# Macaron block on eight cores: the LayerNorm's bf16 cast from GpSimd to VectorE, and a seventh weight slot

## The chip, the cores and the metric

The kernel runs on the eight cores of one Trainium2 chip. Each core works on four of the 32 sequences and exchanges nothing with the others. The metric is the device time of the slowest core in microseconds (us). In this text PE is TensorE, DVE is VectorE, ACT is ScalarE, POOL is GpSimd and SP is SyncE, which issues most of the DMAs.

## The reference

`x` has 32 sequences of 2048 tokens with 1024 channels. The block is half an FFN, attention with latent heads, and half an FFN again, each on the LayerNorm of `x` and added to `x`:

```python
x = x + 0.5 * ffn(layernorm(x), weight, disha)
x = x + attn(layernorm(x), ...)
x = x + 0.5 * ffn(layernorm(x), weight, disha)

def layernorm(x, eps=1e-5):
    m = mean(x); v = var(x)
    return (x - m) / sqrt(v + eps)

def ffn(x, weight, disha):            # r = 64
    result = einsum('bsd,od->bso', x, weight)
    pooled = x.reshape(..., D // r, r).sum(axis=-2)
    return result + pooled @ disha
```

`attn` makes q, k and v with 16 heads of 64, maps each to 32 latent dimensions, rotates q and k, takes a causal softmax and projects back.

## The kernel before

**Layout.** Channels lie on the 128 partitions, in eight chunks of 128, tokens in the columns. A core works on one half sequence at a time (`hb`, 1024 tokens), eight times in all. The half's `x` stays in `x_sb` as float32. Every stage outside attention works on tiles of 512 tokens, `tt` = 0 and 1.

**Stages of one half sequence.** LayerNorm of tile 0, first FFN of tile 0, LayerNorm, attention projection (`emit_cattn`) of tile 0, then the same for tile 1; attention over 16 heads in pairs; the output projection (`emit_cproj`) in two segments of 512 columns; the second FFN in two passes, tile 0 and tile 1, with `store=True`. In the second FFN the result goes through the two halves of `stg` to HBM, and POOL issues the DMA that brings the next half sequence's `x` into the place that has become free (L649).

**A group.** An FFN stage has eight output chunks `o`. Each is a group of eight matmuls into one of two PSUM banks, over the eight input chunks in `ln_sb`. DVE then empties the bank and adds `x` (L657 in the first FFN, L632 in the second, L1011 in the output projection). The attention projection has sixteen such groups, `m` = 0 to 15: 0 to 3 are q, 4 to 7 k, 8 to 15 v. What follows on a group there (rope, norms, transposes of v) is put off by two groups. The v bias row is L789, the copies of the transposed v are L812.

**LayerNorm.** `ln_stats_chunk` does one chunk: a cast of `x` to bf16 into `xb_sb` (L555), its square into one of two halves of `sq_sb` (L558), and two matmuls with a column of ones that sum both over the channels (L563 and L568). `ln_finish` makes mean and scale from the sums (L575 to L600) and writes `ln_sb` in two DVE rows per chunk (L603, L607). The statistics of the next LayerNorm are woven into the stage before it: behind group `o` stands chunk `o - 3`, and the chunks 5, 6 and 7 follow the last group:

```python
            if ln_next is not None and o >= 3:
                ln_stats_chunk(ln_next, o - 3, sqb=lnbank)
        if ln_next is not None:
            ln_stats_chunk(ln_next, 5, sqb=lnbank)
            ln_stats_chunk(ln_next, 6, sqb=lnbank)
            ln_stats_chunk(ln_next, 7, sqb=lnbank)
```

In the attention projection of tile 0 the chunk `m - 8` stands ahead of group `m`, for `m` from 8 on. Six stages of a half sequence carry such chunks: both tiles of the first FFN, the projection of tile 0, the second segment of the output projection, and both passes of the second FFN (in the last half sequence only the first of them, as nothing follows).

**Order and waits.** There is no scheduler. Each engine runs its instructions in the order in which the program writes them. The class `Prog` keeps, for every tile, the last writer and its readers, and puts waits on semaphores ahead of an instruction that needs them. An engine has one semaphore that counts its finished instructions.

**Weights.** `stream_slot` loads the weights of one group (256 KB) over SP's queue into the next of `NSLOT` slots of `wslot`; a load waits until the group that used the slot before is done. Each slot has a semaphore of its own (`SL0`, ...).

Of the kernel before, what the change touches and what calls it, by code (L numbers as in the profile page):

```python
# [38 lines left out]
class Prog:  # L39
# [6 lines left out]
                 "ST0", "ST1", "ST2", "ST3", "ST4", "ST5", "ST6", "ST7",  # L46
                 "PF0", "PF1", "PF2", "PF3", "PF4", "PF5", "PF6", "PF7",
                 "PE", "DV", "AC", "PL",
                 "SL0", "SL1", "SL2", "SL3", "SL4", "SL5")

    def __init__(self):
        self.streams = {e: [] for e in self.ENGINES}
# [146 lines left out]
def build_program(bpc, seq):  # L199
# [49 lines left out]
    def sb(name, shape, dt):  # L249
        return st.enter_context(nc.sbuf_tensor(name, shape, dt))  # L250
# [35 lines left out]
    r_sb = sb("r_sb", [1, 2 * QW], F32)  # L286
    r_bf = sb("r_bf", [1, 2 * QW], BF16)
    rb_sb = sb("rb_sb", [64, 2 * QW], BF16)
    NSLOT = 6
    wslot = sb("wslot", [128, NSLOT * 1024], BF16)  # L290
    stg = sb("stg", [128, 1024], F32)
    build_sb = sb("build_sb", [128, 1024], BF16)
# [47 lines left out]
    p = Prog()  # L340
    BK = [p.R("bank", i) for i in range(8)]

    def bank_ap(i, lo, hi):
        return PS[:, 512 * i + lo:512 * i + hi]
# [3 lines left out]
    def stream_slot(src_ap, src_res):  # L348
        j = slot_ctr[0] % NSLOT
        slot_ctr[0] += 1  # L350
        r = p.R("slot", j)
        p.op("sync", lambda eng, s=src_ap, j=j: eng.dma_start(
            out=wslot[:, 1024 * j:1024 * j + 1024], in_=s),
            reads=[src_res], writes=[r], dma="SL%d" % j)
        return j, r
# [191 lines left out]
    def x_ap(o, hb_local_cols):  # L547
        lo, hi = hb_local_cols
        return x_sb[:, HALF * o + lo:HALF * o + hi]

    def ln_stats_chunk(tt, c, sqb=6):
        g0 = TTA * tt
        par = c % 2
        xres = p.R("x", c, tt)
        p.op("gpsimd", lambda eng, c=c, g0=g0: eng.tensor_copy(  # L555
            xb_sb[:, TTA * c:TTA * c + TTA], x_ap(c, (g0, g0 + TTA))),
            reads=[xres], writes=[p.R("xb", c)])
        p.op("gpsimd", lambda eng, c=c, par=par: eng.tensor_tensor(  # L558
            sq_sb[:, TTA * par:TTA * par + TTA],
            xb_sb[:, TTA * c:TTA * c + TTA],  # L560
            xb_sb[:, TTA * c:TTA * c + TTA], ALU.mult),
            reads=[p.R("xb", c)], writes=[p.R("sq", par)])
        p.group("tensor", [lambda eng, c=c: eng.matmul(  # L563
            bank_ap(0, 0, TTA)[0:1, :], ones128_sb[:],
            xb_sb[:, TTA * c:TTA * c + TTA],
            start=(c == 0), stop=(c == NCH - 1))],
            reads=[p.R("xb", c), p.R("ones128")], writes=[BK[0]])
        p.group("tensor", [lambda eng, c=c, par=par, sqb=sqb: eng.matmul(  # L568
            bank_ap(sqb, 0, TTA)[0:1, :], ones128_sb[:],
            sq_sb[:, TTA * par:TTA * par + TTA],  # L570
            start=(c == 0), stop=(c == NCH - 1))],
            reads=[p.R("sq", par), p.R("ones128")], writes=[BK[sqb]])
# [41 lines left out]
    def emit_ffn(b, hb, tt, ln_next=None, lnbank=6, store=False, nxt=None):  # L614
        g0 = TTA * tt
        for o in range(NCH):
# [11 lines left out]
            if store:  # L628
# [15 lines left out]
                if nxt is not None:  # L644
                    if tt == NT - 1 and o >= 3:
                        ln_stats_chunk(0, o - 3, sqb=3)
                    nb2, nhb2 = nxt
                    p.op("gpsimd", lambda eng, b2=nb2, hb2=nhb2, o=o, g0=g0:
                         eng.dma_start(  # L649
                             out=x_sb[:, HALF * o + g0:HALF * o + g0 + TTA],  # L650
                             in_=d_x[b2, 128 * o:128 * o + 128,
                                     HALF * hb2 + g0:HALF * hb2 + g0 + TTA]),
                         writes=[p.R("x", o, tt)],
                         dma="PF")
# [6 lines left out]
# [6 lines that stand above are left out]
# [499 lines left out]
def run(inputs, bpc, seq, n_cores):  # L1166
    x = np.asarray(inputs["L0_attn_x"], dtype=np.float32)
    B = x.shape[0]
    assert B == bpc * n_cores
    sh = _prep_shared(inputs, seq)  # L1170
    nc = build_program(bpc, seq)
    in_maps = []
    for c in range(n_cores):
        m = dict(sh)
        m["x"] = np.ascontiguousarray(
            x[bpc * c:bpc * (c + 1)].transpose(0, 2, 1))
        in_maps.append(m)
    res = run_bass_kernel_spmd(nc, in_maps, core_ids=list(range(n_cores)))
    outs = [np.asarray(r["out"]) for r in res.results]
    out = np.concatenate(outs, axis=0)  # L1180
    return np.ascontiguousarray(out.transpose(0, 2, 1))
# [4 lines left out]
```

How the kernel before makes its waits and increments, by code:

```python
        def body(eng):  # L180
            for e in stream:
                if e[0] == "w":
                    eng.wait_ge(sems[e[1]], e[2])
                else:
                    ins = e[1](eng)
                    if e[2] is not None:
                        ins.then_inc(sems[e[2]], e[3])
# [923 lines left out]
        def body(eng):  # L1111
            for e in stream:
                if e[0] == "w":
                    eng.wait_ge(sems[e[1]], e[2])
                else:
                    ins = e[1](eng)
                    if e[2] is not None:
                        ins.then_inc(sems[e[2]], e[3])
```

## Time and profile before

| what | us |
|---|---|
| timed runs | 5708.12 and 5788.53 |
| their median | 5748.33 |
| the profiled execution's own time | 5726.87 |
| its span on the slowest core (core 1) | 5725.3 |
| spans of the eight cores | 5683.0 to 5725.3 |

The span reaches from the first to the last instruction on one core, and the execution's own time is that of the slowest core with what lies around it, 1.6 us here. All views are of core 1. Its span holds about 410 us of start (weights are folded and written back to HBM in the order in which they are streamed later), and eight half sequences. "Idle before" in a row is the time for which the engine stood still just ahead of it, with what ended the wait.

### The profile page before, as it was taken

The page shows a single profiled execution, that of the slowest core. Times are in us where ns is not written, and L with a number is a line of the kernel's source. Part 1 is how long each engine was busy: PE and PEld are TensorE (multiplying, and loading weights), DVE is VectorE, ACT ScalarE, POOL GpSimd, SP SyncE. Part 2 cuts the span into 40 slices and gives each one's busy share as a digit, 9 for nine tenths or more (in the row PEclk, how much of TensorE's full clock was granted, in tenths as well). Part 3 has the DMA queues.
Part 4 walks back from the last instruction along what each step waited for, and adds up shares of the span by engine and source line. Part 5 has one row for each costly group of instructions (what it writes and reads, how often), then busy time and mean ns, then how long its engine had stood idle before and what let it go on. Part 6 is the DMA issues. An engine that isn't in the chain of part 4 may idle for free.

```text
span 5725.3 us, 58087 instructions; the slowest of 8 cores (5683.0 to 5725.3 us)
## 1 busy us (share of the span) xinstructions
PE 3783.0 (66%) x13322; PEld 1183.6 (21%) x13322; DVE 1944.4 (34%) x4078; ACT 1671.6 (29%) x1938; POOL 694.0 (12%) x884
## 2 busy tenths in 40 slices
PE   0116666677776666667776666667776666676877
PEld 0002212222221212122221222122221221122222
DVE  1115432531124433451123533352123543253113
ACT  0000350026620052007630043005650035003662
POOL 0012002200022101310013100310003200320001
PEclk9996657776676756786776756677667765776667
DMA  3241003210022102210012101310003100311002
GB/s 86 66 141 50 30 1 104 62 45 1 1 74 81 56 1 63 89 53 7 1 49 94 57 12 30 107 57 17 1 15 111 57 28 3 119 58 31 1 1 78
DMA packets 152516, 277.09 MB, mean 48 GB/s; under 512 B 34322, under 2 KB 34322, under 8 KB 152210
## 3 DMA queue, kind: packets, MB, share of 16 engines
q1 hardware_dynamic: 124818, 210.44, 12.6%
q0 software_dynamic: 8960, 29.37, 1.7%
q10 hardware_dynamic: 18432, 33.56, 1.6%
q8 instruction: 148, 2.42, 0.2%
q14 instruction: 158, 1.29, 0.1%
HBM read 231.36 MB, written 46.14 MB: 48 GB/s over the span
## 4 chain that ended last, share of the span: by engine, by line
PE 48%; DVE 16%; issue 15%; ACT 10%; DMA 6%; POOL 3%; SPq 1%; DVEq 1%; ACTq 0%; POOLq 0%
PE PS L907 12%; PE PS L868 11%; PE PS L621 8%; PE PS L693 7%; ACT PT L880 4%; PE PS L1001 4%; DVE ln_sb L603 3%; DMA stg<-w_attn 3%; DVE rb_sb L953 3%; ACT r_sb L928 2%; POOL sq_sb L558 2%; DVE y_sb L958 1%; PE PS L568 1%; PE PS L563 1%; PE PS L802 1%
## 5 line engine op out<-in xcount | busy, mean ns | idle before, releaser
L880 ACT ACTIVATE PT<-PS,b_exp 128x1024 bf16<-128x1024 f32 (+7 forms) x1536 | 1254.6, 863 | 718.3 <-PE PS L868 691.3
L907 PE MATMUL PS<-PT,v_store 128*65 128x512 bf16 (+3 forms) x2560 | 927.9, 480 | 228.1 <-DVE y_sb L958 207.9
L868 PE MATMUL PS<-q_store,k_store 32*128 32x512 bf16 (+3 forms) x2560 | 772.0, 475 | 325.9 <-ACT PT L880 308.3
L621 PE MATMUL PS<-ln_sb,wslot 128*128 128x512 bf16 x2048 | 676.1, 475 | 176.8 <-DVE ln_sb L607 139.4
L886 DVE TENSOR_TENSOR PT<-PT,causal_sb 128x128 bf16<-128x128 bf16 x1024 | 230.9, 226 | 1504.3 <-ACT PT L880 1495.2
L693 PE MATMUL PS<-ln_sb,wslot 128*128 128x512 bf16 x2048 | 645.1, 463 | 91.8 <-DVE ln_sb L607 91.8
L555 POOL CAST xb_sb<-x_sb 128x512 bf16<-128x512 f32 x384 | 244.8, 637 | 3568.0 <-DVE x_sb L1011 2746.4
L575 ACT ACTIVATE m_bf<-PS 1x512 bf16<-1x512 f32 x48 | 28.2, 587 | 1876.3 <-PE PS L563 1843.6
L558 POOL TENSOR_TENSOR sq_sb<-xb_sb 128x512 bf16<-128x512 bf16 x384 | 399.3, 1040 | 951.1 <-PE PS L568 910.1
L907 PEld LDWEIGHTS PS<-PT,v_store 128*65 128x65 bf16 x2560 | 292.2, 136 | 777.3 <-issue 709.6
L868 PEld LDWEIGHTS PS<-q_store,k_store 32*128 32x128 bf16 x2560 | 180.7, 98 | 927.3 <-issue 905.2
L621 PEld LDWEIGHTS PS<-ln_sb,wslot 128*128 128x128 bf16 x2048 | 219.5, 112 | 611.8 <-issue 517.4
L693 PEld LDWEIGHTS PS<-ln_sb,wslot 128*128 128x128 bf16 x2048 | 209.9, 111 | 466.7 <-issue 353.5
L1001 PE MATMUL PS<-y_sb,wslot 128*128 128x512 bf16 x1024 | 246.9, 399 | 42.6 <-DVE y_sb L958 31.7
L953 DVE CAST rb_sb<-PS 64x1024 bf16<-64x1024 f32 x128 | 157.0, 1227 | 298.8 <-PE PS L947 295.9
L563 PE MATMUL PS<-xb_sb,ones_sb 128*1 128x512 bf16 x384 | 161.8, 421 | 138.5 <-POOL xb_sb L555 133.1
L568 PE MATMUL PS<-sq_sb,ones_sb 128*1 128x512 bf16 x384 | 167.4, 436 | 117.6 <-POOL sq_sb L558 116.7
L632 DVE SCALAR_TENSOR_TENSOR stg<-PS,x_sb 128x512 f32<-128x512 f32 x128 | 88.6, 692 | 419.4 <-PE PS L621 361.5
L749 ACT ACTIVATE sqq_sb<-PS 128x512 bf16<-128x512 f32 x64 | 38.2, 597 | 540.5 <-DVE q_store L744 540.5
L607 DVE TENSOR_TENSOR ln_sb<-ln_sb,ab_sb 128x512 bf16<-128x512 bf16 x384 | 176.0, 458 | 41.0 <-DVE ln_sb L603 1.4
L603 DVE TENSOR_TENSOR ln_sb<-xb_sb,mb_sb 128x512 bf16<-128x512 bf16 x384 | 172.0, 448 | 0.2
L657 DVE SCALAR_TENSOR_TENSOR x_sb<-PS,x_sb 128x512 f32<-128x512 f32 x128 | 88.5, 692 | 236.2 <-PE PS L621 234.2
(103 smaller groups left out, 2241.3 us busy)
## 6 DMA issues: line engine op xcount, KB each, us to landing
wslot<-me_strm SPq DMA_DIRECT2D x256, 256.0 KB, 2.7
wslot<-wa_strm SPq DMA_DIRECT2D x256, 256.0 KB, 2.5
wslot<-cp_strm SPq DMA_DIRECT2D x128, 256.0 KB, 2.6
out<-stg ACTq DMA_DIRECT2D x128, 256.0 KB, 3.1
x_sb<-x POOLq DMA_DIRECT2D x112, 256.0 KB, 4.2
stg<-w_attn SPq DMA_DIRECT2D x48, 256.0 KB
x_sb<-x SPq DMA_DIRECT2D x8, 512.0 KB
wa_strm<-build_sb SPq DMA_DIRECT2D x16, 256.0 KB
```

The costliest lines, as they stand in the source:

```text
L555: p.op("gpsimd", lambda eng, c=c, g0=g0: eng.tensor_copy(xb_sb[:, TTA * c:TTA * c + TTA], x_ap(c, (g0, g0 + TTA))), reads=[xres], writes=[ ...
L558: p.op("gpsimd", lambda eng, c=c, par=par: eng.tensor_tensor(sq_sb[:, TTA * par:TTA * par + TTA], xb_sb[:, TTA * c:TTA * c + TTA], xb_sb[: ...
L568: p.group("tensor", [lambda eng, c=c, par=par, sqb=sqb: eng.matmul(bank_ap(sqb, 0, TTA)[0:1, :], ones128_sb[:], sq_sb[:, TTA * par:TTA * p ...
L603: p.op("vector", lambda eng, c=c: eng.tensor_tensor(ln_sb[:, TTA * c:TTA * c + TTA], xb_sb[:, TTA * c:TTA * c + TTA], mb_sb[:], ALU.subtract),
L621: fns.append(lambda eng, j=j, dd=dd, bk=bk: eng.matmul(bank_ap(bk, 0, TTA), slot_ap(j, dd), ln_sb[:, TTA * dd:TTA * dd + TTA], start=(dd = ...
L693: fns.append(lambda eng, j=j, dd=dd, bk=bk: eng.matmul(bank_ap(bk, 0, TTA), slot_ap(j, dd), ln_sb[:, TTA * dd:TTA * dd + TTA], start=(dd = ...
L868: hg=hg, gq=gq: eng.matmul(PS[:, 1024 * par + a:1024 * par + bnd], k_store[32 * hg:32 * hg + 32, seq * gq + 128 * c:seq * gq + 128 * c + 128],
L880: eng.activation(PT[:, QW * slot + qoff:QW * slot + QW], PS[:, 1024 * par + qoff:1024 * par + QW], AF.Exp, bias=b_exp[:, 0:1]),
L886: p.op("vector", lambda eng, slot=slot, qoff=qoff: eng.tensor_tensor(PT[:, QW * slot + qoff:QW * slot + qoff + 128], PT[:, QW * slot + qof ...
L907: yb=yb: eng.matmul(PS[0:65, yb + a:yb + bnd], v_store[:, 1040 * c + 65 * h:1040 * c + 65 * h + 65], PT[:, QW * slot + a:QW * slot + bnd], ...
L953: p.op("vector", lambda eng, yb=yb, par=par: eng.tensor_copy(rb_sb[:, QW * par:QW * par + QW], PS[64:128, yb:yb + QW]), reads=ybanks, writ ...
L1001: eng.matmul(bank_ap(bk, 0, hi - lo), slot_ap(j, dd), y_sb[:, QW * dd + lo:QW * dd + hi], start=(dd == 0), stop=(dd == NCH - 1)))
```

## The change

The cast of `ln_stats_chunk` is issued on DVE in place of POOL. The square stays on POOL. `NSLOT` goes from 6 to 7, with a semaphore `SL6` and 2 KB more of SBUF in each partition.

```diff
-                 "SL0", "SL1", "SL2", "SL3", "SL4", "SL5")
+                 "SL0", "SL1", "SL2", "SL3", "SL4", "SL5", "SL6")
...
-    NSLOT = 6
+    NSLOT = 7
...
-        p.op("gpsimd", lambda eng, c=c, g0=g0: eng.tensor_copy(
+        p.op("vector", lambda eng, c=c, g0=g0: eng.tensor_copy(
             xb_sb[:, TTA * c:TTA * c + TTA], x_ap(c, (g0, g0 + TTA))),
             reads=[xres], writes=[p.R("xb", c)])
```

DVE's queue in the first FFN stage (tile 0 of the first half sequence), before; the words in brackets are the semaphores that a row waits for (PE, DV, AC and PL are those of the engines, PF that of a prefetch of `x`):

```order
L657 SCALAR_TENSOR_TENSOR x_sb<-PS,x_sb 128x512 [waits PE] x8
L578 TENSOR_TENSOR msq<-m_bf 1x512 [waits AC]
L581 SCALAR_TENSOR_TENSOR var_f<-PS,msq 1x512 [waits PE,DV]
L598 CAST mb_sb<-PS 128x512 [waits PE]
```

The same place now:

```order
L657 SCALAR_TENSOR_TENSOR x_sb<-PS,x_sb 128x512 [waits PE] x4
L555 CAST xb_sb<-x_sb 128x512 [waits DV,PL]
L657 SCALAR_TENSOR_TENSOR x_sb<-PS,x_sb 128x512 [waits PE]
L555 CAST xb_sb<-x_sb 128x512 [waits DV,PL]
L657 SCALAR_TENSOR_TENSOR x_sb<-PS,x_sb 128x512 [waits PE]
L555 CAST xb_sb<-x_sb 128x512 [waits DV,PL]
L657 SCALAR_TENSOR_TENSOR x_sb<-PS,x_sb 128x512 [waits PE]
L555 CAST xb_sb<-x_sb 128x512 [waits DV,PL]
L657 SCALAR_TENSOR_TENSOR x_sb<-PS,x_sb 128x512 [waits PE]
L555 CAST xb_sb<-x_sb 128x512 [waits DV,PL] x4
L578 TENSOR_TENSOR msq<-m_bf 1x512 [waits AC]
```

A cast stands behind the emptying of each bank from the fourth on, and four stand behind the last one. PE's queue keeps its order.

PE's queue there, in the changed kernel, around the group behind the first statistics:

```order
L621 MATMUL PS<-ln_sb,wslot 128x512 x7
L563 MATMUL PS<-xb_sb,ones_sb 1x512 [waits DV]
L568 MATMUL PS<-sq_sb,ones_sb 1x512 [waits PL]
L621 MATMUL PS<-ln_sb,wslot 128x512 [waits SL0,PE]
L621 MATMUL PS<-ln_sb,wslot 128x512 x7
```

The first statistics matmul waits for DVE's semaphore, where it waited for POOL's, and the next group stands behind both.

POOL's queue in the first pass of the second FFN, before, from the first four prefetches on:

```order
L649 DMA x_sb<-x 128x512 [waits DV] x4
L555 CAST xb_sb<-x_sb 128x512
L558 TENSOR_TENSOR sq_sb<-xb_sb 128x512 [waits PL,PE]
L649 DMA x_sb<-x 128x512 [waits DV]
L555 CAST xb_sb<-x_sb 128x512
L558 TENSOR_TENSOR sq_sb<-xb_sb 128x512 [waits PL,PE]
```

The same place now:

```order
L649 DMA x_sb<-x 128x512 [waits DV] x4
L558 TENSOR_TENSOR sq_sb<-xb_sb 128x512 [waits DV,PL,PE]
L649 DMA x_sb<-x 128x512 [waits DV]
L558 TENSOR_TENSOR sq_sb<-xb_sb 128x512 [waits DV,PL,PE]
L649 DMA x_sb<-x 128x512 [waits DV]
```

The casts have left the queue, and each square waits for DVE besides.

## Rows read from the trace of the kernel before

**Rows 1.** The page, first part: busy us, share of the span, instructions.
```profile
PE 3783.0 (66%) x13322; PEld 1183.6 (21%) x13322; DVE 1944.4 (34%) x4078; ACT 1671.6 (29%) x1938; POOL 694.0 (12%) x884
```
**Rows 2.** Who waited for whom: us in total, times, longest us.
```profile
POOL sq_sb L558 <- PE PS L568: 910.1, 201, 271.7
...
PE PS L568 <- POOL sq_sb L558: 116.7, 158, 1.5
...
PE PS L621 <- DMA wslot<-me_strm: 36.9, 1, 36.9
```
**Rows 3.** Timeline, first FFN of tile 0: start, duration, row, idle before.
```profile
423.76 2.28 PE L621 MATMUL PS<-ln_sb,wslot 128*128 128x512 bf16 x8
...
424.32 1.04 POOL L558 TENSOR_TENSOR sq_sb<-xb_sb 128x512 bf16<-128x512 bf16 x1 [1.67 <-DVE x_sb L657]
...
426.14 0.69 DVE L657 SCALAR_TENSOR_TENSOR x_sb<-PS,x_sb 128x512 f32<-128x512 f32 x1 [2.13 <-PE PS L621]
426.21 0.44 PE L568 MATMUL PS<-sq_sb,ones_sb 128*1 128x512 bf16 x1
...
426.58 2.27 PE L621 MATMUL PS<-ln_sb,wslot 128*128 128x512 bf16 x8
```
**Rows 4.** Timeline, end of the same stage.
```profile
434.60 0.69 DVE L657 SCALAR_TENSOR_TENSOR x_sb<-PS,x_sb 128x512 f32<-128x512 f32 x1 [2.13 <-PE PS L621]
...
437.06 1.04 POOL L558 TENSOR_TENSOR sq_sb<-xb_sb 128x512 bf16<-128x512 bf16 x1 [0.21 <-PE PS L568]
...
438.35 0.42 PE L568 MATMUL PS<-sq_sb,ones_sb 128*1 128x512 bf16 x1 [0.82 <-POOL sq_sb L558]
```
**Rows 5.** Groups by line: busy us, mean ns of one, idle before.
```profile
L555 POOL CAST xb_sb<-x_sb 128x512 bf16<-128x512 f32 x384 | 244.8, 637 | 3568.0 <-DVE x_sb L1011 2746.4 <-DVE x_sb L657 457.9 <-DVE c_eff L992 304.1
...
L607 DVE TENSOR_TENSOR ln_sb<-ln_sb,ab_sb 128x512 bf16<-128x512 bf16 x384 | 176.0, 458 | 41.0 <-DVE ln_sb L603 1.4
...
L527 DVE CAST build_sb<-stg 128x1024 bf16<-128x1024 f32 x8 | 5.6, 694 | 36.1 <-DMA stg<-cprojT 36.1
```
**Rows 6.** Windows, DVE rows that write `ln_sb`: length, DVE busy, PEclk, DMA.
```profile
377.00:385.00 8.00, 6.18 (x16) 1.00 0.54 122
443.00:453.10 10.10, 8.48 (x16) 0.50 0.00 1
```
**Rows 7.** Window, line L693 alone, q groups: PE busy, PEld busy, PEclk, DMA.
```profile
462.00:487.50 25.50, 14.80 (x40) 4.48 (x40) 0.65 0.14 42
```
**Rows 8.** Timeline, second FFN, first pass.
```profile
937.93 0.58 POOL L649 DMA_DIRECT2D x_sb<-x  x1 [5.27 <-DVE stg L632]
938.51 0.62 POOL L555 CAST xb_sb<-x_sb 128x512 bf16<-128x512 f32 x1
939.34 1.03 POOL L558 TENSOR_TENSOR sq_sb<-xb_sb 128x512 bf16<-128x512 bf16 x1 [0.21 <-POOL xb_sb L555]
...
941.14 3.59 PE L621 MATMUL PS<-ln_sb,wslot 128*128 128x512 bf16 x8
```
**Rows 9.** Timeline, attention projection of tile 0, around `m` = 8.
```profile
489.46 2.28 PE L693 MATMUL PS<-ln_sb,wslot 128*128 128x512 bf16 x8
...
491.83 0.65 DVE L764 TENSOR_TENSOR k_store<-t_sb 128x512 bf16<-128x512 bf16 x1
```
**Rows 10.** The same stage, a v group.
```profile
512.64 0.74 DVE L789 TENSOR_SCALAR v_sb<-PS,b_vo 128x512 bf16<-128x512 f32 x1
512.80 2.27 PE L693 MATMUL PS<-ln_sb,wslot 128*128 128x512 bf16 x8
```
**Rows 11.** Windows: length, busy of PE, PEld, DVE, ACT, POOL, PEclk, DMA.
```profile
1138.00:1166.00 28.00, 23.46 (x80) 7.27 (x80) 12.18 (x24) 0.59 (x1) 12.85 (x16) 0.80 0.28 76
1057.00:1133.00 76.00, 51.50 (x232) 17.82 (x232) 47.58 (x97) 2.98 (x5) 13.25 (x16) 0.81 0.20 56
...
1663.00:1720.00 57.00, 34.35 (x80) 9.03 (x80) 10.95 (x23) 0.59 (x1) 17.54 (x24) 0.58 0.35 111
1726.00:1765.00 39.00, 27.35 (x81) 7.98 (x81) 11.49 (x24) 0.59 (x1) 17.60 (x24) 0.72 0.55 176
```

The windows are, in this order: first FFN of tile 1, attention projection of tile 0 and, of the second half sequence, first and second pass of the second FFN.

## The prediction

> **What bounds the kernel now.** I began with the page's first part: POOL is busy for 12% of the span [rows 1], so an engine-by-engine share would call its load harmless, and moving the 384 casts a matter of taste. The view of who waited for whom says where to look instead: POOL's square waits 910.1 us in 201 places for TensorE's own statistics matmul, and TensorE waits only 116.7 us in 158 places for the square [rows 2]. So POOL runs ahead of TensorE and stands waiting for a free square buffer (there are two). The timeline of one FFN stage shows this in detail [rows 3]: the square of a later chunk starts at 424.32, while TensorE is still in the group of 423.76. When the group is done, the two statistics matmuls (the second at 426.21) find their inputs ready, and the next group of eight follows at 426.58, which is 0.44 us after VectorE began to empty the bank of the group before (426.14). TensorE is the bound inside these stages, and the statistics cost it only their own matmuls. What lets POOL run ahead is that its queue holds only statistics (and, in the second FFN, prefetches): a cast there starts as soon as its x chunk exists, whatever VectorE has still to do.
>
> **What the change does to that order.** A chunk's statistics (number o-3) stand behind group o in the program. On VectorE the cast now stands behind the emptying of group o's bank, which waits for TensorE to end group o. POOL's square waits for the cast, TensorE's second statistics matmul waits for the square, and group o+1 stands behind that matmul. A chain that was loose by three groups becomes a closed ring: group, emptying, cast, square, statistics, next group.
>
> **An ordinary FFN stage, step by step.** From the start of the emptying: 0.69 for it [rows 3], 0.43 for the cast, 0.2 to hand over to POOL (the gap of 0.21 ahead of the square of 437.06 [rows 4]), 1.04 for the square [rows 3], 0.25 from its end to the matmul (437.06 + 1.04 to 438.35 [rows 4]), and 0.37 from that matmul to the next group (426.21 to 426.58 [rows 3]). That is 2.98 us, where 0.44 stands now: 2.5 us more per group.
> The cast's price on VectorE is not in the trace for this tile. The same conversion between the same memories for 1024 columns takes 694 ns [rows 5]; halved it is 0.35, undivided 0.69. I take 0.43, between the half and the 458 ns that VectorE's multiply of a 128x512 tile takes [rows 5], and keep both ends.
> Four of the five stalled groups (o = 3 to 6) delay a group: 4 x 2.5 = 10.0 us. Behind o = 7 come the casts and squares of chunks 4 to 7. Today the last square starts 2.46 us after the last emptying began and its matmul 3.75 us after it [rows 4], because POOL had only two chunks left. Now all four squares come behind the first cast: 0.69 + 0.43 + 0.2 + 4 x 1.04 + 0.25 = 5.7, or 2.0 more.
>
> **Shared memory port.** The sixteen normalising rows of a LayerNorm took 6.18 us with POOL idle, and 8.48 us with POOL casting beside them [rows 6]. In the tail VectorE's casts of chunks 5 to 7 now meet POOL's squares. If they only queue politely it costs nothing; if a cast waits for a square each time, three casts add up to 3 x 0.4 = 1.2 us. I take 0.8 for each tail. The same rows give something back: ahead of the attention projection of tile 0 those casts are gone, and with them 8.48 - 6.18 = 2.3 us.
> The Trainium skill, SBUF — State Buffer, section "SBUF: two separate sides", says that VectorE and GpSimd share a port pair as an exclusive lock that is held for the whole instruction. The 2.3 us [rows 6] agree. By that rule alone each tail would pay the full 1.2 us instead of 0.8, some 16 us more over the kernel.
>
> **TensorE's clock.** A ring of 5.3 us with 2.3 us of group in it looks like today's q part of the attention projection, where five groups (40 matmuls) stand in 25.5 us. They took 14.80 us of it at a granted clock of 0.65 [rows 7], 2.96 us per group, against 2.28 in the FFN stage [rows 3]. So the chip went back and forth between its two levels, 1.2 and 2.4 GHz, and I charge 0.7 us for each delayed group. The ends are 0 (it stays at the upper level) and 1.3 (the lower one throughout: 3.59 us per group [rows 8]).
>
> **Sums for one half sequence (there are 8).**
> First FFN, both token tiles, and the output projection's second segment, three stages of one kind: 4 x (2.5 + 0.7) + 2.0 + 0.8 = 15.6 us each, 46.8.
> Attention projection of tile 0: eight chunks, from m = 8 on. For m = 8 the cast stands behind the rope work of m = 7, whose last row starts at 491.83; the next VectorE row could start about 0.55 later, so the group comes at 492.4 + 0.43 + 0.2 + 1.04 + 0.25 + 0.37 = 494.7, where it is 489.46 now [rows 9]: 5.2. For the other seven, from the start of the v bias row: 0.74 + 0.43 + 0.2 + 1.04 + 0.25 + 0.37 = 3.0 where 0.16 stands now [rows 10]: 2.8 each, 19.6. With 8 x 0.7 for the clock and 2.3 back: 28.1.
> Second FFN, first pass: here the ring exists already, since POOL must first issue the prefetch of x, which waits for the emptying: issue 0.58, cast with its hand-over 0.83, square, all in a row on POOL [rows 8]. The cast leaves that row: -0.83 for each of five chunks, and -0.8 for each of the last three, -6.5; with 0.8 for the port, -5.7.
> Second FFN, second pass: 39 us now at a clock of 0.72 [rows 11]. It becomes a stage like the first FFN's after the change: 28 + 15.6 = 43.6 [rows 11], and the emptying, which now holds TensorE up, waits at times for a store; +6, from 0 to +10.
> Together 75.2, times 8 is 602. In the last half sequence nothing is prefetched: its first pass gains no 5.7 but loses 15.6, and the second pass has no statistics: 602 + 21.3 - 6 = 617 us.
>
> **What costs nothing.** The seventh weight slot: TensorE waited for a weight load once, 36.9 us before the first FFN, for the first load [rows 2]; one more load in flight shortens no wait. At the start of the program the casts come behind VectorE's weight folding, some 12 us later than now (an estimate: eight squares of 1.04 us in a row, with their hand-overs), and that same 36.9 us wait covers them; without it they would cost those 12 us. Attention holds no cast at all.
>
> **Total.** The profiled execution ran 5726.9 us (span 5725.3); the two timed runs gave 5708.1 and 5788.5, median 5748.3, so the sum stands on a run from their lower part. 5726.9 + 617 = 6344; I say 6340.
> Bounds: 24 stalled groups and chunks per half sequence, 192 in all. The cast at 0.35 or 0.69: -15 or +50. The clock, 160 groups, 0 or 1.3: -112 or +96. The port, 40 tails, 0 or 1.2: -32 or +16. The second pass: -42 or +28. All low 6143, all high 6534.
>
> **Rivals.**
> Full clock: TensorE keeps the upper level through the rings. For it: the attention projection as a whole ran at 0.81 [rows 11]. Against it: [rows 7]. 6340 - 112 - 20 (second passes) = 6208, say 6210. Chance 0.20.
> Low clock: the ring holds TensorE at 1.2 GHz as the first pass of the second FFN is held now (clock 0.58 [rows 11], groups of 3.59 us). 6340 + 96 = 6436. Chance 0.18.
> Faster, by the second FFN: that first pass takes 57 us where the first FFN's stage takes 28 for the same matmuls [rows 11]. If POOL, rid of the casts, no longer held it up, 29 x 7 = 203 us would go. This wins from the point where a ring costs less than 203 / 192 = 1.06 us per group instead of 2.5, that is, if the casts could slip in ahead of the emptying. With 0.4 us per group (the cast alone) the time is 5727 - 203 + 77 = 5600. Against it: the prefetch issue stays on POOL, behind the emptying [rows 8], and the cast cannot pass a row ahead of it. Chance 0.03.
> The Trainium skill, GPSIMD Engine Reference, section "Key points", calls VectorE structurally about twice as fast for elementwise work. The trace agrees on the single cast (637 ns on POOL, 694 for twice the columns on VectorE [rows 5]), and that is the argument for this rival.
> No change: the squares' chain is hidden after all and gains and losses cancel, 5727. For it: POOL's large idle share [rows 1]. Chance 0.03.
> A ring as worked out here, with a mixed clock, has 0.56; its own range is 6260 to 6420.
>
> **Numbers.** Slower by over 2% (about what can be told from no change) holds the forecast and both clock rivals, 0.94; within 2% 0.03; faster 0.03. The range 6160 to 6490 takes in both clocks and most of the bounds; attention may also shift by itself, for which I have no price.
>
> **What would show it.** In the changed profile the wait of the statistics matmul L568 for the square should be the largest of TensorE's (some 192 waits of about 1 us), with one for the cast beside it. The emptying should be followed by the cast, the square and the group at 0.7, 1.3 and 3.0 us. The FFN stage should take 43 us instead of 28, the projection of tile 0 104 instead of 76, the first pass 51 instead of 57, attention the same. The forecast is wrong if TensorE starts a group while the square before it still runs, or if the first pass falls to 30 us.

## The result, and the profile after

The changed kernel takes 6494.9 us (median of 11 runs, 6473.6 to 6520.5), the kernel before 5730.1 us (10 runs, 5708.1 to 5788.5). The ratio is 1.132, with an interval from 1.128 to 1.136: 765 us slower. In some executions of any of these kernels the cores of one die show a lower granted clock and the time is about 1% longer; the times and ratios of all runs below are medians of the other executions. Direction and mechanism came as forecast. The size did not: 6495 lies 155 us above the predicted 6340 and 5 us above the upper end of the range.

The page's first part, as in [rows 1] (engine, busy us, share of the span, instructions; some matmul records are missing):

```profile
span 6492.0 us, 57942 instructions; the slowest of 8 cores (6447.4 to 6492.0 us)
...
PE 4070.5 (63%) x13176; PEld 1247.6 (19%) x13322; DVE 2092.4 (32%) x4462; ACT 1670.6 (26%) x1938; POOL 472.2 (7%) x500
```

VectorE got 148 us of work more, POOL 222 less, and no engine is near full. Yet TensorE, which had no instruction added, is busy for at least 287 us more. Its matmuls became longer.

Who waited for whom, as in [rows 2] (us in total, times, longest us):

```profile
POOL sq_sb L558 <- DVE xb_sb L555: 5523.8, 224, 481.4
...
PE PS L563 <- DVE xb_sb L555: 516.1, 260, 89.5
...
PE PS L568 <- POOL sq_sb L558: 263.9, 283, 1.6
```

Before, the square waited for TensorE, which had not yet read the square ahead of it. Now it waits for the cast, and TensorE waits for both. Before TensorE's first statistics matmul the emptying and the cast go by, before its second one the square. One of the 260 waits for the cast, the longest, is not of a ring: it stands at the start of the program, where VectorE folds weights first.

The timeline of the first FFN of tile 0, one ring and the end of the stage (start, duration, row, idle before):

```profile
440.06 0.69 DVE L657 SCALAR_TENSOR_TENSOR x_sb<-PS,x_sb 128x512 f32<-128x512 f32 x1 [4.93 <-PE PS L621]
...
440.67 0.42 DVE L555 CAST xb_sb<-x_sb 128x512 bf16<-128x512 f32 x1
...
441.36 1.04 POOL L558 TENSOR_TENSOR sq_sb<-xb_sb 128x512 bf16<-128x512 bf16 x1 [4.92 <-DVE xb_sb L555]
...
442.65 0.59 PE L568 MATMUL PS<-sq_sb,ones_sb 128*1 128x512 bf16 x1 [0.72 <-POOL sq_sb L558]
...
443.17 3.60 PE L621 MATMUL PS<-ln_sb,wslot 128*128 128x512 bf16 x8
...
446.87 0.69 DVE L657 SCALAR_TENSOR_TENSOR x_sb<-PS,x_sb 128x512 f32<-128x512 f32 x1 [5.78 <-PE PS L621]
...
447.48 2.27 DVE L555 CAST xb_sb<-x_sb 128x512 bf16<-128x512 f32 x4
...
448.16 4.50 POOL L558 TENSOR_TENSOR sq_sb<-xb_sb 128x512 bf16<-128x512 bf16 x4 [5.76 <-DVE xb_sb L555]
...
452.91 0.59 PE L568 MATMUL PS<-sq_sb,ones_sb 128*1 128x512 bf16 x1
```

From the start of the emptying to the cast it is 0.6 us, to the square 1.3, to the next group 3.11: the ring, where [rows 3] have 0.44 us. The group in it takes 3.60 us instead of 2.28. The period, from emptying to emptying, is 6.8 us.

Windows, as in [rows 11] (length; busy of PE, PEld, DVE, ACT, POOL; PEclk; DMA share; GB/s): first FFN of tile 1, attention projection of tile 0, second FFN's first and second pass.

```profile
1274.00:1322.30 48.30, 33.05 (x79) 8.92 (x80) 15.23 (x31) 0.79 (x2) 8.65 (x8) 0.57 0.15 44
1158.00:1269.10 111.10, 66.82 (x228) 21.05 (x231) 46.89 (x102) 3.11 (x6) 8.31 (x8) 0.67 0.13 38
1822.40:1872.60 50.20, 31.64 (x79) 9.15 (x81) 15.67 (x31) 0.59 (x1) 12.93 (x16) 0.70 0.40 126
1878.70:1928.50 49.80, 34.16 (x80) 9.04 (x81) 14.56 (x32) 0.59 (x1) 12.77 (x16) 0.57 0.47 138
```

The first FFN's stage went from a clock of 0.80 to 0.57, the projection from 0.81 to 0.67, the second pass from 0.72 to 0.57. The first pass, which had a ring before, went from 0.58 to 0.70. These are single stages, and the first FFN's 0.57 is the lowest of its eight in tile 1. The mean over the first seven half sequences went from 0.78 and 0.79 (first FFN, tile 0 and tile 1) to 0.70 and 0.67, from 0.79 to 0.67 in the projection of tile 0, from 0.75 to 0.59 in the second pass, and from 0.61 to 0.67 in the first.

With every stage's length read from TensorE's rows, mean over half sequences 2 to 8 (the last half sequence, in which nothing is prefetched, is in them; without it the first pass went from 57.4 to 51.3 us and the second from 38.2 to 50.1):

| stage, us | before | after | early cast (E3) | statistics first (E4) | both (E5) |
|---|---|---|---|---|---|
| first FFN, tile 0 | 29.2 | 46.8 | 27.5 | 28.4 | 28.7 |
| projection, tile 0 | 77.2 | 112.5 | 75.8 | 76.6 | 75.6 |
| first FFN, tile 1 | 28.1 | 46.5 | 27.3 | 28.1 | 28.6 |
| projection, tile 1 | 74.5 | 73.9 | 74.1 | 73.9 | 74.4 |
| output projection | 36.7 | 55.7 | 36.1 | 36.6 | 38.1 |
| second FFN, first pass | 53.6 | 50.9 | 47.6 | 36.0 | 33.3 |
| second FFN, second pass | 36.2 | 46.5 | 32.5 | 37.2 | 33.4 |

The differences between the first two columns add up to 97.3 us, times 8 is 778. The first half sequence lost less, 77 us, so that all eight give 759. The normalisations between the stages took 21 us more, and attention, 2356 us in all before and 2341 after, takes 15 off: with 1 us at the start that is the 767 us between the two profiled spans. The stages that carry casts are nearly all of it; the projection of tile 1, which carries none, stayed. Attention's 15 us are no gain that can be told: among the cores of the kernel before it differs by 26 us.

### The profile page after: what moved, and what is told of

Read it like the earlier page. It is cut to its first block, busy times and chain, and to the rows that moved or that the text cites. A ratio compares the mean times of both kernels' runs of the same rounds, so it can differ in the third digit from the quotient of the medians.

```text
span 6492.0 us, 57942 instructions; the slowest of 8 cores (6447.4 to 6492.0 us)
## 1 busy us (share of the span) xinstructions
PE 4070.5 (63%) x13176; PEld 1247.6 (19%) x13322; DVE 2092.4 (32%) x4462; ACT 1670.6 (26%) x1938; POOL 472.2 (7%) x500
## 4 chain that ended last, share of the span: by engine, by line
PE 47%; DVE 18%; issue 15%; ACT 9%; DMA 5%; POOL 4%; SPq 1%; DVEq 1%; ACTq 0%; POOLq 0%
PE PS L907 10%; PE PS L621 9%; PE PS L868 9%; PE PS L693 7%; PE PS L1001 4%; POOL sq_sb L558 4%; ACT PT L880 4%; PE PS L568 3%; DMA stg<-w_attn 3%; DVE ln_sb L607 2%; DVE rb_sb L953 2%; DVE ln_sb L603 2%; ACT r_sb L928 2%; DVE xb_sb L555 2%; DVE y_sb L958 1%
## 5 line engine op out<-in xcount | busy, mean ns | idle before, releaser
L907 PE MATMUL PS<-PT,v_store 128*65 128x512 bf16 (+3 forms) x2560 | 910.9, 472 | 227.6 <-DVE y_sb L958 208.1
L621 PE MATMUL PS<-ln_sb,wslot 128*128 128x512 bf16 x1993 | 773.3, 543 | 184.2 <-DVE ln_sb L607 148.7
L558 POOL TENSOR_TENSOR sq_sb<-xb_sb 128x512 bf16<-128x512 bf16 x384 | 410.4, 1078 | 5532.4 <-DVE xb_sb L555 5523.8
L693 PE MATMUL PS<-ln_sb,wslot 128*128 128x512 bf16 x1984 | 708.3, 509 | 83.2 <-DVE ln_sb L607 71.0
L575 ACT ACTIVATE m_bf<-PS 1x512 bf16<-1x512 f32 x48 | 28.1, 586 | 2748.4 <-PE PS L563 2748.4
L563 PE MATMUL PS<-xb_sb,ones_sb 128*1 128x512 bf16 x384 | 191.6, 499 | 516.1 <-DVE xb_sb L555 516.1
L568 PE MATMUL PS<-sq_sb,ones_sb 128*1 128x512 bf16 x384 | 204.6, 533 | 268.7 <-POOL sq_sb L558 263.9
L621 PEld LDWEIGHTS PS<-ln_sb,wslot 128*128 128x128 bf16 x2048 | 243.4, 124 | 658.6 <-issue 591.5
L693 PEld LDWEIGHTS PS<-ln_sb,wslot 128*128 128x128 bf16 x2048 | 226.9, 119 | 495.0 <-issue 410.6
L1001 PE MATMUL PS<-y_sb,wslot 128*128 128x512 bf16 x997 | 287.9, 452 | 46.5 <-DVE y_sb L958 34.3
L812 DVE COPY v_store<-PS 128x256 bf16<-128x256 bf16 x256 | 75.2, 294 | 424.6 <-PE PS L802 424.2
L555 DVE CAST xb_sb<-x_sb 128x512 bf16<-128x512 f32 x384 | 197.4, 542 | 0.9 <-issue 0.8
L1011 DVE SCALAR_TENSOR_TENSOR x_sb<-PS,c_eff,x_sb 128x512 f32<-128x512 f32 x128 | 96.1, 751 | 295.2 <-PE PS L1001 270.5
```

The source lines that it names most:

```text
L555: p.op("vector", lambda eng, c=c, g0=g0: eng.tensor_copy(xb_sb[:, TTA * c:TTA * c + TTA], x_ap(c, (g0, g0 + TTA))), reads=[xres], writes=[ ...
L558: p.op("gpsimd", lambda eng, c=c, par=par: eng.tensor_tensor(sq_sb[:, TTA * par:TTA * par + TTA], xb_sb[:, TTA * c:TTA * c + TTA], xb_sb[: ...
L621: fns.append(lambda eng, j=j, dd=dd, bk=bk: eng.matmul(bank_ap(bk, 0, TTA), slot_ap(j, dd), ln_sb[:, TTA * dd:TTA * dd + TTA], start=(dd = ...
L693: fns.append(lambda eng, j=j, dd=dd, bk=bk: eng.matmul(bank_ap(bk, 0, TTA), slot_ap(j, dd), ln_sb[:, TTA * dd:TTA * dd + TTA], start=(dd = ...
L907: yb=yb: eng.matmul(PS[0:65, yb + a:yb + bnd], v_store[:, 1040 * c + 65 * h:1040 * c + 65 * h + 65], PT[:, QW * slot + a:QW * slot + bnd], ...
L1001: eng.matmul(bank_ap(bk, 0, hi - lo), slot_ap(j, dd), y_sb[:, QW * dd + lo:QW * dd + hi], start=(dd == 0), stop=(dd == NCH - 1)))
```

## The experiments

The theory: the cast's place in VectorE's queue, behind an emptying that waits for TensorE, closes a ring, and the ring also costs clock. The rivals: the seventh slot has a part in it; VectorE has too much work or shares its port with POOL; the ring's clock costs as little as I had charged, and the rest is somewhere else.

**E1, the cast alone, and E2, the slot alone.**

```diff
# E1, from the changed kernel
-    NSLOT = 7
+    NSLOT = 6
# E2, from the changed kernel
-        p.op("vector", lambda eng, c=c, g0=g0: eng.tensor_copy(
+        p.op("gpsimd", lambda eng, c=c, g0=g0: eng.tensor_copy(
```

> The cast on VectorE with six weight slots as before. Ring theory (each group's statistics wait for emptying, cast and square in a row): all of the loss is the cast's, so 6495 us within 20, and FFN stages of 46 us as in the changed kernel. Rival (the seventh slot changes when weights land and costs or gives something): more than 30 us away from 6495.

> The seventh weight slot with the cast on POOL as before. Ring theory: 5730 us within 20, since no group waited for a weight load after the first. Rival (the slot has a price of its own): more than 30 us away from 5730.

E1 took 6493.3 us, ratio to the kernel before 1.133 (1.128 to 1.137); E2 5731.2 us, 1.0015 (0.998 to 1.005). The cast is the whole loss, and the slot is worth nothing that can be told.

**E3, the cast early.** The changed kernel, with the cast of chunk o right behind the emptying of group o, three groups ahead of its statistics. Casts, squares and matmuls are as many as in the changed kernel, and the casts stay on VectorE; squares and statistics matmuls keep their place. The second FFN and the output projection are done in the same way; `ln_cast` is the cast of `ln_stats_chunk`, split off.

```diff
+    def ln_cast(tt, c):
...
                     reads=[BK[bk], xr], writes=[xr])
+                if ln_next is not None:
+                    ln_cast(ln_next, o)
...
+            if ln_next is not None and 6 <= m < 14:
+                ln_cast(ln_next, m - 6)
             flush(m)
```

> All casts stay on VectorE, but cast c stands right behind the emptying of group c (in the attention projection ahead of the vector work of group c+6), so it is done three groups before TensorE asks for it; the squares and the statistics matmuls stay where they are. Ring theory: the place in the queue is what costs. First FFN stages go back from 46 to 28 us, the projection of tile 0 from 112 to 74, the first pass of the second FFN stays near 51 because the prefetch is still ahead of the square: 5660 us, from 5620 to 5740. Rival (384 more rows on VectorE, or their meeting with POOL at the shared port, are what costs): above 6200.

Measured: 5610.0 us, ratio 0.978 (0.974 to 0.983), 885 us less than the changed kernel with the same work on the same engines. The timeline of a first FFN's stage (E3's line numbers: L663 emptying, L554 cast, L560 square, L570 statistics, L623 group):

```profile
1862.30 0.69 DVE L663 SCALAR_TENSOR_TENSOR x_sb<-PS,x_sb 128x512 f32<-128x512 f32 x1 [0.43 <-PE PS L623]
1862.34 0.38 PE L570 MATMUL PS<-sq_sb,ones_sb 128*1 128x512 bf16 x1
...
1862.65 1.90 PE L623 MATMUL PS<-ln_sb,wslot 128*128 128x512 bf16 x8
1862.87 1.04 POOL L560 TENSOR_TENSOR sq_sb<-xb_sb 128x512 bf16<-128x512 bf16 x1 [2.16 <-PE PS L570]
1863.17 1.02 DVE L554 CAST xb_sb<-x_sb 128x512 bf16<-128x512 f32 x1 [0.17 <-DVE x_sb L663]
```

The next group starts 0.35 us after the emptying began (0.44 before the change [rows 3]), and the group takes 1.90 us: TensorE is at its upper level here. The square now runs beside the group. The cast beside it takes 1.02 us instead of 0.43 and ends 0.28 us after the square: that fits the shared port, for which I had charged 0.8 us in each tail, and here it costs nothing, since nobody waits for this cast.
The Trainium skill, SBUF — State Buffer, section "SBUF: two separate sides", has VectorE and GpSimd exclude each other for a whole instruction, if VectorE's is in a mode that uses two ports or has two inputs in SBUF. A cast that waited for all the rest of the square would have taken 0.74 + 0.43 = 1.17 us, so the trace agrees nearly, at 1.02.

So neither VectorE's load nor its meeting with POOL made the loss. VectorE is busy for longer here (2148 us) than in the changed kernel. The place in the queue made it.
The kernel is even faster than before the change, though the interval leaves open whether by more than 2%. By the table it wins 14.6 us per half sequence, 9.7 of them in the second FFN's passes, where the cast has left POOL's row of prefetch, cast and square; times 8 is 117, and 112 to 120 were measured, by which median of the kernel before is taken (5722.5 us beside this run, 5730.1 in the result above).

**E4, the statistics first.** This one is made from the kernel before, with the cast on POOL, and asks about the ring that was there already, in the second FFN's first pass: the prefetch that POOL must issue behind the emptying, ahead of the cast and the square.

```diff
                 if nxt is not None:
+                    if ln_next is not None and o >= 3:
+                        ln_stats_chunk(ln_next, o - 3, sqb=lnbank)
                     if tt == NT - 1 and o >= 3:
...
-            if ln_next is not None and o >= 3:
+            if ln_next is not None and o >= 3 and nxt is None:
                 ln_stats_chunk(ln_next, o - 3, sqb=lnbank)
```

> The kernel before, with one thing exchanged in the first pass of the second FFN: the statistics of chunk o-3 stand ahead of the prefetch of x for chunk o, as they already do in the second pass. Theory (the prefetch on POOL, which waits for the emptying, closes a ring there): the first pass falls from 57 us to between 30 and 38, 133 to 189 us less in all, 5541 to 5597. Rival (the pass is set by its traffic of stores, prefetches and weights): 57 us as before, 5730.

Measured: 5577.2 us, ratio 0.973 (0.968 to 0.978), 145 to 153 us less than the same two medians of before. The same two passes by windows (first and second pass):

```profile
1633.10:1670.30 37.20, 26.86 (x81) 7.79 (x81) 11.16 (x23) 0.59 (x1) 17.65 (x24) 0.78 0.55 170
1676.00:1715.50 39.50, 27.67 (x81) 7.90 (x81) 11.37 (x24) 0.59 (x1) 17.60 (x24) 0.76 0.55 173
```

The first pass fell from 57 us to 37, its clock rose from 0.58 to 0.78, and POOL did the same work in it (17.6 us [rows 11]).

**E5, both.** E3 and E4 in one kernel.

> Both cures at once: the casts on VectorE right behind the emptying of their group (seven slots), and in the first pass of the second FFN the statistics ahead of the prefetch. Ring theory: the two rings are independent, so the first pass falls from 47.6 us (early casts alone) to the 32.5 us of the second pass, 7 x 15 = 105 us under the 5624 of the early casts alone: 5520 us, from 5480 to 5560. Rival (the traffic of that pass is what is left): no better than the 5582 us of the statistics-first kernel.

Measured: 5491.3 us, ratio 0.959 (0.957 to 0.961), 29 us better than expected. 0.978 times 0.973 is 0.952, below the interval: most of both gains add, but each alone had already taken something out of the first pass (53.6 us to 47.6 in E3, to 36.0 in E4), and that counts once. First and second pass now take 33 us each.

**E6, TensorE kept busy.** The changed kernel, with five matmuls of 512 columns behind each group that a ring follows. Nobody reads their results.

```diff
+            if o >= 3 and (ln_next is not None or nxt is not None):
+                filler(j, 5, 7, lambda i: ln_sb[:, TTA * i:TTA * i + TTA])
...
+            if ln_next is not None and 7 <= m < 15:
+                filler(j, 5, 7, lambda i: ln_sb[:, TTA * i:TTA * i + TTA])
...
+                if si == len(segs) - 1 and o >= 3:
+                    filler(j, 5, 1, lambda i: y_sb[:, QW * i + lo:QW * i + hi])
```

> The changed kernel with five more matmuls of 512 columns behind each group that has a ring, into a PSUM bank nobody reads, while TensorE would wait for the emptying and the cast. Theory (half of the loss beyond the bare waits is TensorE at 1.2 GHz, because it stands still in each ring): the groups in the rings fall from 3.3 us to 1.9 to 2.4, about 218 of them, so the kernel gets faster by doing more: 6255 us, from 6200 to 6330, with granted clocks above 0.8 in the FFN stages. Rival (the clock is low for another reason, or the extra matmuls stand in the way): 6495 us or more.

Measured: 6206.7 us, ratio 1.084 (1.081 to 1.087), 288 us less than the changed kernel, with some 1300 matmuls more. A ring of a first FFN's stage (L665 emptying, L561 cast, L564 square, L574 statistics, L627 group, L552 the added matmuls):

```profile
574.40 1.24 PE L552 MATMUL PS<-ln_sb,wslot 128*128 128x512 bf16 x5
...
574.67 0.69 DVE L665 SCALAR_TENSOR_TENSOR x_sb<-PS,x_sb 128x512 f32<-128x512 f32 x1 [3.77 <-PE PS L627]
...
575.28 0.41 DVE L561 CAST xb_sb<-x_sb 128x512 bf16<-128x512 f32 x1
...
575.96 1.04 POOL L564 TENSOR_TENSOR sq_sb<-xb_sb 128x512 bf16<-128x512 bf16 x1 [3.75 <-DVE xb_sb L561]
...
577.25 0.38 PE L574 MATMUL PS<-sq_sb,ones_sb 128*1 128x512 bf16 x1 [0.93 <-POOL sq_sb L564]
577.56 1.90 PE L627 MATMUL PS<-ln_sb,wslot 128*128 128x512 bf16 x8
```

And a first FFN's stage of tile 1 by window, beside the changed kernel's first window above:

```profile
2022.00:2063.50 41.50, 31.29 (x105) 10.33 (x105) 14.60 (x32) 0.59 (x1) 8.63 (x8) 0.83 0.17 51
```

The ring is the same (emptying to next group 2.89 us; 2.95 in the mean over the changed kernel's first FFNs), but the group takes 1.90 us instead of 3.60, and the granted clock is 0.83 instead of 0.57 (0.84 instead of 0.67 in the mean). The FFN's matmuls by groups of lines (busy us, mean ns of one, idle before), in the changed kernel and in E6:

```profile
L621 PE MATMUL PS<-ln_sb,wslot 128*128 128x512 bf16 x1993 | 773.3, 543 | 184.2 <-DVE ln_sb L607 148.7 <-DMA wslot<-me_strm 28.7 <-issue 5.1
```

```profile
L627 PE MATMUL PS<-ln_sb,wslot 128*128 128x512 bf16 x2048 | 649.9, 460 | 161.1 <-DVE ln_sb L613 135.7 <-DMA wslot<-me_strm 25.4
```

One takes 460 ns instead of 543; in the kernel before it was 475. So what E6 takes off, 288 us, is clock, and 6207 - 5730 = 477 us is left. Of the 288 some 22 lie in first passes, whose ring was there before (the stretch of their groups went from 44.0 us to 40.8, seven times). The clock's part of the loss is thus 266 us, and the rest, 499, is waiting.

**E7, the cast twice.** The changed kernel, with each cast done twice in the same place.

> The changed kernel with each cast on VectorE done twice in a row. Ring theory: every ring gets longer by the whole second cast with its wait for the first, about 0.5 us, in 218 rings: +113 us, 6610, from 6580 to 6650. Rival (casts lie beside TensorE's work): 6495 us within 20, though VectorE is busy for another 165 us.

Measured: 6613.9 us, ratio 1.155 (1.153 to 1.158), 119 us more than the changed kernel. The timeline, the wait that took it up (L558 is the second cast, L566 the first statistics matmul), and a ring of a first pass (L635 emptying, L652 prefetch, L561 square):

```profile
438.22 0.42 DVE L555 CAST xb_sb<-x_sb 128x512 bf16<-128x512 f32 x1
...
438.74 0.43 DVE L558 CAST xb_sb<-x_sb 128x512 bf16<-128x512 f32 x1
```

```profile
PE PS L566 <- DVE xb_sb L558: 670.7, 258, 91.1
```

```profile
1888.26 0.69 DVE L635 SCALAR_TENSOR_TENSOR stg<-PS,x_sb 128x512 f32<-128x512 f32 x1 [5.35 <-PE PS L624]
...
1889.39 0.43 DVE L558 CAST xb_sb<-x_sb 128x512 bf16<-128x512 f32 x1
1889.57 0.58 POOL L652 DMA_DIRECT2D x_sb<-x  x1 [5.30 <-DVE xb_sb L555]
...
1890.17 1.05 POOL L561 TENSOR_TENSOR sq_sb<-xb_sb 128x512 bf16<-128x512 bf16 x1
```

0.52 us from cast to cast times some 220 rings (28 in each half sequence but for the last one's second pass: four in each of five stages, eight in the projection) is 114 us, and the wait for the cast grew by 155. That 114 meets 119 so closely is partly luck, since the rings do not pay alike. From emptying to next group those of the first FFN went from 2.95 us to 3.60, 0.65 in place of 0.52, and a part of that is the clock again: the second statistics matmul ran at the lower level (0.59 us, not 0.38) in 59 of 64 of these rings, in the changed kernel in 23. Those of the first pass stayed at 3.62: there POOL issues the prefetch while the second cast runs, and the square could not start before it. So what is put on VectorE between emptying and square is paid in every ring in which nothing beside it covers it.

**E8, the same remedy in the projection.** E5 with five such unread matmuls in each q step of the attention projection (64 places), where [rows 7] showed a clock of 0.65 in the kernel before.

```diff
                                 reads=[p.R("qp", qpar), p.R("wqk4bf")],
                                 writes=[BK[nb]])
+                        filler(5)
```

> On top of the early casts with the statistics first (5491 us): five matmuls nobody reads in each q step of the attention projection, between the latent product and the norm for which TensorE waits on ScalarE; 64 places. Theory (those waits keep TensorE at 1.2 GHz for about half of the q and k groups, 2.96 us per group against 2.28 or less): 0.7 to 1.0 us less per place, 45 to 64 us, so 5440 us, from 5400 to 5470. Rival (the extra matmuls stand in the way of the norm, or the clock there is held down by something else): 5490 us or more.

Measured: 5460.0 us, ratio 0.9535 (0.950 to 0.957), the best version, though its interval just touches E5's. By the groups of lines (busy us, mean ns of one, idle before), the projection's matmuls in E5 and in E8:

```profile
L703 PE MATMUL PS<-ln_sb,wslot 128*128 128x512 bf16 x2048 | 643.8, 462 | 70.4 <-DVE ln_sb L609 70.4
```

```profile
L712 PE MATMUL PS<-ln_sb,wslot 128*128 128x512 bf16 x2048 | 576.1, 423 | 70.4 <-DVE ln_sb L618 70.4
```

68 us less busy, but only some 30 us less time. The waits show one place where it went: TensorE's wait for the norm of q fell, that for the norm of k rose. First E5's two rows, then E8's:

```profile
PE PS L764 <- ACT sqq_sb L761: 143.9, 64, 3.1
...
PE PS L788 <- DVE sqk_sb L782: 62.7, 47, 2.3
```

```profile
PE PS L775 <- ACT sqq_sb L772: 96.1, 64, 2.0
...
PE PS L799 <- DVE sqk_sb L793: 84.2, 48, 2.3
```

The second grew by 21.5 us: a faster TensorE waits longer for VectorE in the k part. The 320 added matmuls are busy for 80.2 us, more than the 47.8 us by which the wait for the norm of q fell. With the matmuls of the two FFNs, 14 us shorter too (634.4 to 620.1), that makes 68 + 14 + 48 less and 80 + 21.5 more: 28 us, an estimate from one core of each run, and close to what was measured.

## Why the prediction was right, and where it was off

**The ring: right.** Predicted were 2.98 us from emptying to next group, measured 3.11 at the lower clock and 2.89 at the upper one (E6), and 2.95 in the mean of the first FFN's rings. The cast was taken at 0.43 and took 0.42. The tail was put at 5.7 + 0.8 from its emptying to the last statistics matmul, and is 6.04, so that the port's 0.8 was at most 0.3. The 2.3 us that were to come back did: the sixteen normalising rows ahead of the projection of tile 0 took 5.95 us in place of 8.48. The first pass went from 57 us to 51 as worked out. E7 shows that the ring is closed (one cast more lengthens it), E3 that only the place in the queue closes it.

**The clock: the term that was mis-sized.** "I charge 0.7 us for each delayed group" is the step that failed. I took it from the q groups of [rows 7], 2.96 us each, because a ring of 5.3 us with 2.3 us of group in it looked like them. In the changed kernel the groups in the rings took 3.1 to 3.5 us in the mean of each kind of stage, at a mean granted clock of 0.59 to 0.70 in those stages of the FFN and the projection. The length that I compared with was wrong as well: 2.28 us [rows 3] is a group of the first half sequence, and over the whole kernel before, the same groups took 1.9 to 2.1 us in the mean (2.3 in the second pass), most of them 1.90. So a delayed group cost some 1.1 to 1.5 us of clock, not 0.7. A ring of 2.9 us, with a group of matmuls between two of them, holds TensorE at its lower level of 1.2 GHz for most of the stage, as the first pass had been held [rows 8]. That row described this ring more closely, group, emptying, one POOL chain, group, and the "Low clock" rival was drawn from it.
I also counted 160 groups and left the second pass out of this term, which E6 shows to pay as well (the stretch of its groups went from 42.7 us to 37.1, seven times); only its +6 held a little of it. By E6 the clock cost 288 - 22 = 266 us where 160 x 0.7 = 112 were charged. The other terms of the sum came to 617 - 112 = 505, and what is left of the loss is 765 - 266 = 499. So the miss lies in one term, as far as E6 tells the clock's part from the rest. The projection of tile 0 (35 us more per half sequence, not 28) and the second pass (12 us where its statistics are made, not 6) are the same miss read by stage.
The mixed clock was given 0.56 and the low one 0.18. The "Low clock" rival's 6436 was nearer, still 59 us short, of which some 39 are the second pass's groups, which it did not count either.

**What costs nothing: right.** The seventh slot moves nothing (E1, E2). The start of the program came out as said: TensorE's wait for the first weight load, which was to cover the later casts, fell from 36.9 to 28.7 us, and the first group started at 414.8 us instead of 413.4.

**A sign that read otherwise.** I expected TensorE's wait for the square to be its largest. It is 263.9 us in 283 places (0.93 each, as expected in size), but the wait for the cast is larger, 516.1 us in 260 places, or 426.6 without the one of 89.5 at the start of the program: in it stand the emptying's 0.69 us, the cast and the hand-overs, which I had in the sum but had not read as part of TensorE's wait for the cast.

**"Faster, by the second FFN": the gain was real, the route was not.** I had priced the first pass's stall at 29 x 7 = 203 us and said that the cast's going would not free it, because the prefetch issue stays ahead of the square. Both held. E4 took 145 to 153 us of it by moving the statistics ahead of the prefetch, and left the cast on POOL. And the condition that I named for the rival, that "the casts could slip in ahead of the emptying" of the next groups, is what E3 did in the program, with the 0.978 that follows.

## What to carry to other kernels

Before an operation is moved to another engine's queue, look at what stands ahead of it there and for whom that waits: one row of 0.43 us behind an emptying that waits for TensorE cost 765 us, and the same row three groups earlier made the kernel 2% faster than before. If the next engine down the line is TensorE, count each ring twice, once for its waiting and once for the matmuls of the group at 1.2 GHz, and take that price from the stage with the most similar ring. Busy shares tell nothing of this: POOL fell from 12% to 7%, no engine came near its limit, and the two best kernels have VectorE at 39% of the span, the highest share of all.

## What the runs showed of the hardware that I had not expected

More work made the kernel faster: some 1300 matmuls that nobody reads took 288 us off in E6, at 1.24 us for five, and 320 took about 30 us off in E8. Over a third of the price of the stalls on TensorE (266 of 765 us) was in the group that followed: 3.60 us instead of 1.90 behind the same wait. In a first FFN's ring TensorE did not stand still for long at a time: 1.4 us before the first statistics matmul and 0.7 to 0.9 before the second.

VectorE's cast of 128x512 from float32 to bf16 takes 0.42 us alone (0.64 on POOL [rows 5]) and 1.02 beside POOL's square, and its mean over a kernel says more of its neighbours than of itself: 542 ns in the changed kernel, and in E3, where squares and casts meet in every group, 658 ns, in the faster kernel of the two.
